# Attention weights turned by VectorE blocks and quadrant DMAs instead of TensorE transposes, in a two-layer graph attention kernel

## The reference

```python
def _gat_layer(x, W, adj):
    proj = x @ W
    Wh, Ws = jnp.split(proj, 2, axis=-1)
    scores = Wh @ Ws.T
    a = jax.nn.softmax(scores, axis=-1) * adj
    out = a @ Wh
    out = out + x
    return jax.nn.leaky_relu(out, NEG_SLOPE)
...
for l in range(W_stack.shape[0]):
    x = _gat_layer(x, W_stack[l], adj)
return x
...
x = _layernorm(x + _L0_gnn_ref(x, adj, L0_gnn_W_stack), axis=-1)
```

## Time and profile before

| | |
|---|---|
| median of 3 runs | 1793.34 us (1793.21 to 1793.46) |
| span of the profiled execution (first to last instruction) | 1791.6 us |
| median of the runs less that span | 1.7 us |
| busy: PE | 1770.0 us |
| busy: PEld / DVE / ACT / POOL | 1519.4 / 1293.3 / 787.6 / 120.7 us |
| mean granted TensorE clock | 0.998 of 2.4 GHz |
| instructions | 31961 |
| moved by DMA | 196.40 MB, mean 110 GB/s |

### The profile page before, as it was taken

How to read it: one execution, slowest core, us unless ns; L and a number is a source line. 1 busy time by engine, 2 the same in 40 slices (tenths; PEclk the granted TensorE clock), 3 DMA queues, 4 the chain that set the end, 5 groups by cost and what they waited for, 6 DMA issues and landing times.

```text
span 1791.6 us, 31961 instructions
## 1 busy us (share of the span) xinstructions
PE 1770.0 (99%) x10152; PEld 1519.4 (85%) x10152; DVE 1293.3 (72%) x2406; ACT 787.6 (44%) x1767; POOL 120.7 (7%) x199
## 2 busy tenths in 40 slices
PE   8999999999999999999999999999999999999997
PEld 8988888888888888888898888888888888888886
DVE  5677777776777776767666777777777777777776
ACT  5544444444444444444365444444444444444442
POOL 0000000000000000000000001100110010011001
PEclk9999999999999999999999999999999999999999
DMA  6533333233333333333264333333333333333331
GB/s 205 166 105 104 101 100 104 94 103 100 103 99 102 102 105 100 100 105 100 68 230 145 94 118 109 96 103 112 110 99 108 111 111 99 108 111 104 95 113 39
DMA packets 70614, 196.40 MB, mean 110 GB/s; under 512 B 8640, under 2 KB 16832, under 8 KB 70592
## 3 DMA queue, kind: packets, MB, share of 16 engines
q1 hardware_dynamic: 62912, 175.14, 31.3%
q0 software_dynamic: 7680, 20.98, 3.4%
HBM read 171.97 MB, written 24.12 MB: 109 GB/s over the span
## 4 chain that ended last, share of the span: by engine, by line
PE 98%; DVE 1%; DMA 0%; ACT 0%; issue 0%; POOL 0%; SPq 0%; ACTq 0%; DVEq 0%; POOLq 0%
PE banks L429 27%; PE banks L286 15%; PE banks L287 15%; PE banks L288 15%; PE banks L432 13%; PE banks L412 12%; PE banks L321 1%; DMA load<-x_scratch 0%; DVE q_t L553 0%; DMA ring<-w 0%; DVE moving_lo L553 0%; PE banks L296 0%; ACT moving_hi L533 0%; ACT q_t L494 0%; DVE rows L664 0%
## 5 line engine op out<-in xcount | busy, mean ns | idle before, releaser
L429 PE MATMUL banks<-wh,moving_hi 128*128 128x512 f32 x2048 | 787.9, 419 | 0.1
L516 ACT ACTIVATE ring<-banks,neg_max 128x512 f32<-128x512 f32 x512 | 353.0, 690 | 766.3 <-DVE neg_max L607 766.1
L553 DVE TENSOR_TENSOR moving_lo<-banks,moving_hi 128x512 fp32r<-128x512 f32 x545 | 376.9, 691 | 396.3 <-ACT moving_hi L533 393.5
L432 PE MATMUL banks<-wh,moving_lo 128*128 128x256 f32 x2048 | 575.4, 281 | 0.0
L429 PEld LDWEIGHTS banks<-wh,moving_hi 128*128 128x128 f32 x2048 | 385.8, 188 | 70.0 <-DVE moving_lo L553 0.8
L286 PE MATMUL banks<-x_t,q_t 128*128 128x512 f32 x1024 | 404.1, 395 | 0.4 <-DVE q_t L553 0.4
L287 PE MATMUL banks<-x_t,q_t 128*128 128x512 f32 x1024 | 401.4, 392 | 0.0
L288 PE MATMUL banks<-x_t,q_t 128*128 128x512 f32 x1024 | 399.9, 391 | 0.0
L642 DVE SCALAR_TENSOR_TENSOR ring<-ring,weight,load 128x512 f32<-128x512 f32 x512 | 381.3, 745 | 16.6 <-issue 9.0
L432 PEld LDWEIGHTS banks<-wh,moving_lo 128*128 128x128 f32 x2048 | 389.3, 190 | 0.0
L533 ACT ACTIVATE moving_hi<-banks 128x512 fp32r<-128x512 f32 x512 | 306.2, 598 | 176.1 <-PE banks L432 176.1
(11 more groups left out here) (66 smaller groups left out, 791.1 us busy)
## 6 DMA issues: line engine op xcount, KB each, us to landing
load<-adj SPq DMA_DIRECT2D x256, 512.0 KB, 4.0
qt_scratch<-q_t SPq DMA_DIRECT2D x30, 512.0 KB, 3.0
q_t<-qt_scratch SPq DMA_DIRECT2D x60, 256.0 KB, 4.2
load<-x SPq DMA_DIRECT2D x16, 256.0 KB, 3.2
rows<-x POOLq DMA_DIRECT2D x32, 128.0 KB, 4.0
x_scratch<-rows POOLq DMA_DIRECT2D x32, 128.0 KB, 2.0
load<-x_scratch SPq DMA_DIRECT2D x16, 256.0 KB, 3.0
rows<-x_scratch POOLq DMA_DIRECT2D x32, 128.0 KB, 3.4
```

Of the source, the lines that this page charges most:

```text
L429: nc.tensor.matmul(psum[:, bank, :], moving_hi[:, slot % 2, of], wh[:, j].rearrange("p a d -> p (a d)"), start=start, stop=stop, skip_grou ...
L432: last = nc.tensor.matmul(psum[:, bank, 0:D], moving_lo[:, slot % 2, of], wh[:, j, 0], start=False, stop=stop, skip_group_check=True)
L516: nc.scalar.activation(ring[:, slot, :], psum[:, SCORE_BANK + k % SCORE_BANKS, :], ACT.Exp, bias=neg_max[:, slot:slot + 1], accum_out=chun ...
L553: return nc.vector.tensor_tensor(out_ap, value, as_f32(hi), ALU.subtract)
```

## The change

A step is now a chunk of 1024 columns: 4 chunks a tile, 128 steps a layer. The scores of a chunk fill two of four PSUM banks; the maximum, the exponentials and the weighing are one instruction of 1024 each. The four PE transposes of a 512-column chunk are gone. In their place:

- DVE `turn_blocks` (L610) transposes the 32x32 blocks of a chunk in place, right after its weighing;
- SP `move_blocks` (L223) issues eight DMAs for each chunk, each from 32 partitions of `ring` to 32 partitions of `turned` (64 KB). Two chunks make a unit of 2048 columns; a column's partition in `turned` is then another one than before, and the tiles of `wh` are made in that order of columns (`pick_columns`);
- ACT rounds `turned` into `a_hi` (L507), GpSimd subtracts into `a_lo` (L691), 512 columns at a time, both from SBUF to SBUF;
- PE multiplies a chunk 7 steps after its scores (L395, L397).

Before the first step only x is turned (8 groups of 512 rows) and q of the first two tiles made. The 16 wh pairs of a layer (12 matmuls each, "sides") stand in its first steps, for layer 1 eight of them at one step (`LATE_GROUP`) after the last product of layer 0; the other q pairs, one each 8 steps. GpSimd gathers the columns of x_t for each wh pair (four copies of 256 elements, L709). q stays in SBUF. Layer 1's x groups are turned in the four steps between the layers, its last group at `LATE_GROUP`. Rows are loaded and stored from SP. No engine has a loop. M and W of layer 1 are made in the fill, kept in DRAM and loaded at step 120.

```diff
-    CHUNK = 512
-    LAG_WEIGHT = CHUNKS + 1
-    LAG_TRANSPOSE = CHUNKS + 2
+    BANK = 512
+    CHUNK = 2 * BANK
+    RING = 6
+    LAG_WEIGH = 4
+    LAG_PRODUCT = 7
+    LAG_ROWS = 11
+    OFFSET = CHUNKS + 4
+    STEPS = OFFSET + CHUNKS + LAG_ROWS + 3
+    LATE_GROUP = OFFSET + 3
...
+            def move_blocks(i):
+                unit, c = i // 2, i % 2
+                u = unit % 2
+                sp.wait_ge(blocks_turned, i + 1)
+                if unit >= 2:
+                    sp.wait_ge(lo_done, SUB * (unit - 1))
+                for q in range(2 * c, 2 * c + 2):
+                    for r in range(QUADS):
+                        sp.dma_start(as_f32(turned[QUAD * q:QUAD * (q + 1), u, r]).rearrange("p b j -> p (b j)"),
+                                     ring[QUAD * r:QUAD * (r + 1), i % RING, (q - 2 * c) * BANK:(q - 2 * c + 1) * BANK]
+                                     ).then_inc(moved[u][q], 16)
...
+                i = chunk_at(step - LAG_WEIGH)
+                if i is not None:
+                    move_blocks(i)
+                    if i + 2 < LAYERS * CHUNKS:
+                        load_adj(i + 2)
...
-                    for b in range(BLOCKS):
-                        last = nc.tensor.transpose(psum[:, AT_BANK + slot % 2, b * P:(b + 1) * P],
-                                                   ring[:, slot, b * P:(b + 1) * P], ident[:])
-                    last.then_inc(at_done, 1)
...
+            for step in range(STEPS):
+                for side in sides_before(step):
+                    make_side(side)
+                if step == LATE_GROUP:
+                    transpose_x(2 * GROUPS - 1)
+                i = chunk_at(step)
+                if i is not None:
+                    scores(i)
+                k = chunk_at(step - LAG_PRODUCT)
...
+                if k is not None:
+                    product(2 * k)
+                    product(2 * k + 1)
+                for g in x_groups_at(step):
+                    transpose_x(g)
...
+            def exponentials(i):
+                t, c = i // CPT, i % CPT
+                of = t % 2 * CPT + c
+                act.wait_ge(max_done, i + 1)
+                if i >= RING:
+                    m = i - RING
+                    for q in range(2 * (m % 2), 2 * (m % 2) + 2):
+                        act.wait_ge(moved[m // 2 % 2][q], 64 * (m // 4 + 1))
...
+            def split_a(j):
+                unit, b = j // SUB, j % SUB * SUB
+                if b == 0:
+                    for q in range(QUADS):
+                        act.wait_ge(moved[unit % 2][q], 64 * (unit // 2 + 1))
+                if j % SUBS < 2:
+                    act.wait_ge(side_done, side_place["wh", j // SUBS * WPAIRS + WPAIRS - 1] + 1)
+                else:
+                    act.wait_ge(product_done, j - 1)
+                nc.scalar.activation(a_hi[:, j % 2].rearrange("p b (r j) -> p b r j", r=QUADS),
+                                     as_f32(turned[:, unit % 2, :, b:b + SUB, :]).rearrange("p r b j -> p b r j"),
+                                     ACT.Copy).then_inc(hi_done, 1)
...
+            def turn_blocks(i):
+                dve.wait_ge(a_done, i + 1)
+                nc.vector.transpose(ring[:, i % RING, :], ring[:, i % RING, :]).then_inc(blocks_turned, 1)
...
+            def split_a(j):
+                unit, b = j // SUB, j % SUB * SUB
+                pool.wait_ge(hi_done, j + 1)
+                nc.gpsimd.tensor_tensor(
+                    a_lo[:, j % 2].rearrange("p b (r j) -> p b r j", r=QUADS),
+                    as_f32(turned[:, unit % 2, :, b:b + SUB, :]).rearrange("p r b j -> p b r j"),
+                    as_f32(a_hi[:, j % 2]).rearrange("p b (r j) -> p b r j", r=QUADS),
+                    ALU.subtract).then_inc(lo_done, 1)
```

More of the change, by code:

```diff
@@ L157, in as_f32 @@
             return ap.bitcast(F32)
[L159 to L196, removed]
+        def chunk_at(step):
+            for layer in range(LAYERS):
+                if 0 <= step - layer * OFFSET < CHUNKS:
+                    return layer * CHUNKS + step - layer * OFFSET
+            return None
@@ new lines, in tile_at, with x_groups_at, sides_before @@
+        def tile_at(step):
+            for layer in range(LAYERS):
+                n = step - layer * OFFSET
+                if n >= 0 and n % CPT == 0 and n // CPT < TILES:
+                    return layer * TILES + n // CPT
+            return None
+        def x_groups_at(step):
+            n = step - CHUNKS
+            if 0 <= n < 4:
+                return [GROUPS + g for g in range(2 * n, min(2 * n + 2, GROUPS - 1))]
+            return []
+        def sides_before(step):
+            return [("wh", WPAIRS + v) for v in range(WPAIRS // 2)] if step == LATE_GROUP else []
@@ L281, in _ @@
+            for p in range(2):
+                sp.wait_ge(rows_stored[p], 16 * TILES)
         @block.tensor
@@ new lines, in product @@
+            def product(j):
+                layer, m = j // SUBS, j % SUBS
+                t, of_tile = layer * TILES + m // SUBS_TILE, m % SUBS_TILE
+                bank, s = ACC_BANK + t % 2, j % 2
+                if m == 0:
+                    pe.wait_ge(side_lo, side_place["wh", layer * WPAIRS + WPAIRS - 1] + 1)
+                if of_tile == 0 and t >= 2:
+                    pe.wait_ge(acc_free, t - 1)
+                pe.wait_ge(lo_done, j + 1)
+                for b in range(SUB):
+                    k = of_tile * SUB + b
+                    start, stop = k == 0, k == TILES - 1
+                    nc.tensor.matmul(psum[:, bank, :], a_hi[:, s, b], wh[:, k].rearrange("p a d -> p (a d)"),
+                                     start=start, stop=stop, skip_group_check=True)
+                    last = nc.tensor.matmul(psum[:, bank, 0:D], a_lo[:, s, b], wh[:, k, 0],
+                                            start=False, stop=stop, skip_group_check=True)
+                last.then_inc(product_done, 1)
@@ new lines, in _ @@
+            for step in range(STEPS):
+                ready, done, last = tile_at(step - CPT), tile_at(step - LAG_ROWS), tile_at(step - LAG_ROWS - 1)
+                late = step == LATE_GROUP
+                if ready is not None:
+                    row_weights(ready)
+                if late:
+                    finish_rows(done)
+                i = chunk_at(step - LAG_WEIGH)
+                if i is not None:
+                    weigh(i)
+                    turn_blocks(i)
+                for side in sides_before(step):
+                    split_side(side)
+                if late:
+                    split_x(2 * GROUPS - 1)
+                for g in x_groups_at(step):
+                    split_x(g)
+                i = chunk_at(step)
+                if i is not None:
+                    chunk_max(i)
+                for side in sides_after(step):
+                    split_side(side)
+                if last is not None and last >= TILES:
+                    normalise_rows(last)
+                if done is not None and not late:
+                    finish_rows(done)
```

828 lines of the change are left out of this document (401 added, 427 removed).

## The result

The changed kernel takes **1897.09 us** (median of 3 runs, 1891.64 to 1900.65), the one before 1793.34: a ratio of 1.0575, with a 95% interval of 1.0549 to 1.0601. It is 103.7 us slower, and 269 us above the predicted 1628.0.

What follows compares the result with a forecast made beforehand. PE was taken to bound the kernel: 1545 us of work, idle of 12.5, 4.5, 21 and 14.5, and 29 of layer 1 stalls gave a 1626.5 us span, 1628 as measured time; range 1580 to 1745.

Steps and rivals of the forecast that it cites:

- PE's work: PE busy time over the whole kernel: 1770.0 less 225 us of weight transposes, so 1545 us; 5.58 us a step.
- Instruction fetch, at nothing: Fetching 7973 PE instruction rows instead of 1366 was costed at nothing, being under the steps' slack.
- Rival 3: In VectorE's turning, the block transpose takes two passes, 2.2 us: 77 us more, 1704 us; chance 0.11.
- nine a step are 3.1 to 5.2 us ... All under 5.58: SP's nine DMA issues a step, at 0.34 to 0.58 us each, were said to fit into PE's 5.58 us step.
- Rival 2: SP's DMA issues bind the steps: with waits for turning T = 6.3 us a step, 1739 us; chance 0.07.
- the formula 256 T + 126: Predicted span in us if something other than PE binds each of 256 steps at T us.
- In layer 0, finish_rows being 1.3, nothing: At a tile's first step in layer 0, VectorE's row work was said to cause PE no stall: 0 us.
- The 29 us of layer 1: PE stalls at layer 1 tile starts, since finish_rows stands ahead of the maximum: 0.9 us a tile, 32 tiles.
- Rival 4, the exclusion: VectorE's weighing and GpSimd's subtraction exclude each other, each weighing waiting 1.17 us: 37 us more, 1664 us; chance 0.12.
- DVE 19.3 us of a layer 1 tile against 23.0: VectorE's summed work in a layer 1 tile, 19.3 us, was said to fit within PE's 23.0 us.
- Idle elsewhere: PE idle outside the steps: fill 12.5, step 7 4.5, between the layers 21, drain 14.5 us.
- Rival 1, the bytes: The 32-partition moves bind the DMA engines: at three times the cost T = 7.0 us, span 1918 us; chance 0.09.

Runs made afterwards that it cites:

- e17: e8 with layer 1's residual, statistics, 1/std and normalising left out, so its row work is that of layer 0: 1646.1 us, one run.
- e8: Changed kernel with adjacency load ahead, one 128-partition move a chunk (columns land wrong) and a tile's first maximum ahead of weighing and turning: 1697.0 us.
- e6: e1 with GpSimd filling the weights' low part with zeros instead of subtracting: 1733.8 us, one run.
- e1: Changed kernel with the adjacency load issued ahead of the eight moves, once weighing has freed its buffer: 1762.5 us, ratio 0.9833 to the kernel before.
- e3: Changed kernel with each of the eight moves taking half the columns, 32 KB instead of 64 KB: 1880.6 us, one run.
- e2: Changed kernel with one 128-partition move a chunk instead of eight, same bytes, columns in wrong places, load still behind it: 1746.9 us, one run.
- e12: e8 with GpSimd's 1/std put behind the step's two subtractions instead of ahead of them: 1696.2 us, ratio 0.9461 to the kernel before.

## Why the prediction was wrong

The gap of 269 us (1897.1 - 1628), in the order in which edits closed it: the one move instead of eight 150 (1746.9), the first maximum ahead 50 (1697.0), layer 1's row work 51 (1646.1). What is left is 18. But e17 leaves out the work for which the forecast held 29 us of stalls, so 47 us are still to be found: 38 in PE's busy time, 9 in stalls of layer 1 that stay in e17 (8.8 us idle from 900 to 1600). The shares follow this order of the edits; in another order they would be others.

- *PE's work*: right for a step, short as a sum. Score blocks start 300.00 and 305.60 in e17, a step of 5.60 us where 5.58 was said. But PE is busy 1583.1 us in e17, not 1545: some 15 of the 38 are the clock (below), 5 the 0.02 of each step, the rest was not taken apart. In the changed kernel, where PE waits in most steps, the same instructions keep it busy 1648.5 us (L395 423 ns in the mean, 405 in e17; clock 0.971 and 0.988).
- *Instruction fetch, at nothing*: not refuted. From 100 to 780 us of e17 PE is busy all 680.
- *Prices of VectorE, ScalarE, GpSimd alone*: right. Maximum 1191 ns (1.22 said), weighing 1.28 where nothing runs beside it, block transpose 1245 ns (1.2), rounding 625 (633), subtraction 2.53 us for two, so 1.27 (1.17). Rival 3 falls.
- *"Nine a step are 3.1 to 5.2 us ... All under 5.58"*: **the step that failed.** The issue cost 0.59 us with a gap of 0.04, so nine are 5.6 us and not under 5.58; but the error that cost most was to compare them as a rate with a step. The adjacency load stood behind eight issues and had two buffers, so issues, landing (4.9 us) and VectorE's 3.2 us add up to 13.1 for two steps. Rival 2 is this place, and its price too low: it gave T = 6.3 and 1739, where the loop gives 6.55 and, by the formula 256 T + 126, 1803. The weighings in fact stand 6.81 us apart in the mean in both layers (chunks 32 to 112, 144 to 240), which makes 1869; that the 0.26 come from the tile's first steps below, which the loop doesn't let catch up, is argued. The last 30 us of the span are outside the steps or the formula's own error; no run parts them.
- *"In layer 0, finish_rows being 1.3, nothing"*: wrong. The same count as for layer 1 needs the small multiplication at 1.29 us, not 0.2, and the weighing at 2.27, not 1.28. With these, the maximum is late in layer 0 too. Putting it first gave 50 us (e8), nearly all in layer 0, a term that the sum had at nothing.
- *The 29 us of layer 1*: right in kind, too small. Leaving out that row work gave 51.
- *Rival 4, the exclusion*: the mechanism is there and mis-sized from both sides: it lengthens the weighing by 1.0 us at times, 0.34 us in the mean (1624 against 1281 ns), not all by 1.17, and a 128x4 multiplication from 0.23 to 1.29 us. Its price was 37 us; e6 gives 29, with another limit close behind. The Trainium skill ("SBUF — State Buffer", Who interferes with whom) says that a VectorE instruction with two SBUF inputs and a GpSimd one that reads SBUF shut each other out. The trace agrees (1281 ns with a GpSimd that only writes, 1624 with one that reads).
- *"DVE 19.3 us of a layer 1 tile against 23.0"*: right as a sum (76.64 of 100 us in e1, so 19.7 of a tile's 25.7) and no proof. What counts is the distance between two maxima, and that was 8 us.
- *Idle elsewhere*, in e17: fill 12.5 said, 12.0; step 7 4.5 said, 7.9 (60 to 100 us); between the layers 21 said, 21 (780 to 900); drain 14.5 said, 11. The sum, 52.5, is right in part by luck, since two errors cancel. *"I take no cost from [the clock]"*: wrong, small. In e17 the granted clock, a mean of 2.4 and 1.2 GHz, is 0.83 from 60 to 100 us and 0.83 to 0.91 in most slices from 780 to 900, each after PE had idled in or just before them; PE's busy time in each slice times what the clock lacks there comes to some 15 us.
- *Rival 1, the bytes*: falls with e3.

## What to carry over

A cost in a queue is a rate only where nothing in the queue feeds the loop that fills it: list what stands behind each group of DMA issues, and close the loop by hand (issues + landing + work, divided by the buffers) before comparing with a step. Put the loads that someone waits for ahead of stores and moves: that one order was worth 135 us here. It makes this change 1.7% faster than the kernel before (e1) where it was 5.8% slower. And an edit can cost 15 us beside one limit and give 50 without it; when two limits stand at nearly the same height, test them lifted together.

## What was not expected of the hardware

- An issue in a row takes SP 0.59 us plus a gap of 0.04, for the 64 KB of a move and the 32 KB of e3 alike, and 0.58 for the 512 KB of a load behind them. It isn't a constant: the four loads in a row before took 0.43 to 0.83, the rows' transfers of the kernel after 0.43 to 0.46 (medians).
- A VectorE multiplication of 128x4 elements by a scalar takes 0.23 us alone and 1.29 where it starts beside a GpSimd subtraction: in e2 from 409.96 to 411.25, while the first of the two subtractions runs from 409.94 to 411.23. The tensor-tensor operations of 0.16 to 0.17 us in that stretch end before the subtraction starts; beside one, in e12, the addition of one element (L631, 1409.84) takes 0.70 in place of 0.16.
- The power of one element on GpSimd took 550 ns after the change and 987 before; no run here was made to find out why.
- A store of 512 KB to DRAM took 6.2 us to land with an adjacency load just ahead of it, where 512 KB between parts of SBUF took 3.8.
